# A transformer block on one core: values two groups behind the scores, the first half of the output projection between the last two, and the next layer norm moved ahead of the feed-forward

## The reference

```python
x = x + _L0_xattn_ref(_layernorm(x), ctx, ctx, Wq, Wk, Wv, Wo, lam, g)
x = x + _L0_ffn_ref(_layernorm(x), ln1_g, ln1_b, w1, b1, ln2_g, ln2_b, w2, b2)
```

## Time and profile before

| | us |
|---|---|
| median of 3 runs (2399.65 to 2402.44) | 2401.85 |
| the profiled execution's own time | 2400.83 |
| its span, first to last instruction | 2399.0 |
| busy: TensorE / VectorE / ScalarE / GpSimd | 2150.0 / 1804.7 / 1510.4 / 1047.7 |
| mean granted share of TensorE's clock | 0.953 |

### The profile page before, as it was taken

How to read it: one execution, slowest core, us unless ns; L and a number is a source line. 1 busy time by engine, 2 the same in 40 slices (tenths; PEclk the granted TensorE clock), 3 DMA queues, 4 the chain that set the end, 5 groups by cost and what they waited for, 6 DMA issues and landing times.

```text
span 2399.0 us, 45089 instructions
## 1 busy us (share of the span) xinstructions
PE 2150.0 (90%) x18239; PEld 1188.0 (50%) x18239; DVE 1804.7 (75%) x2722; ACT 1510.4 (63%) x1973; POOL 1047.7 (44%) x803
## 2 busy tenths in 40 slices
PE   7777899999899999999999999999989899999978
PEld 5444455554455555454545545455544545555443
DVE  4676778777787878778787878878687777867763
ACT  3575676656577665657766565766756576675644
POOL 2301715437182543718154371816346181634507
PEclk9868999999899999999999999999999999999989
DMA  8313113130411314031141303122141312312010
GB/s 292 109 47 81 44 55 80 24 108 22 112 47 54 80 24 108 23 98 46 54 95 25 108 22 97 46 71 72 37 104 20 97 46 70 72 37 72 2 53 18
DMA packets 253007, 160.14 MB, mean 67 GB/s; under 512 B 171812, under 2 KB 221580, under 8 KB 252288
## 3 DMA queue, kind: packets, MB, share of 16 engines
q1 hardware_dynamic: 249792, 152.07, 24.4%
q0 software_dynamic: 3008, 5.20, 0.7%
HBM read 51.82 MB, written 20.38 MB: 30 GB/s over the span
## 4 chain that ended last, share of the span: by engine, by line
PE 46%; POOL 23%; DVE 13%; ACT 8%; issue 5%; DMA 3%; SPq 1%; POOLq 0%; DVEq 0%; ACTq 0%
POOL attn_raw L684 21%; PE ps L1613 10%; PE ps L1444 5%; PE ps L1445 5%; PE ps L1597 5%; PE ps L1446 5%; DVE attn_raw L1143 3%; PE ps L1532 3%; DVE arena L1272 2%; DMA rows<-attn_raw 2%; ACT arena L808 2%; ACT attn_raw L811 2%; DVE attn_raw L1157 1%; ACT arena L806 1%; POOL attn_raw L680 1%
## 5 line engine op out<-in xcount | busy, mean ns | idle before, releaser
L684 POOL TENSOR_TENSOR attn_raw<-attn_raw 128x512 f32<-128x512 f32 x448 | 658.1, 1488 | 47.9 <-ACT attn_raw L836 18.1
L662 POOL TENSOR_TENSOR q<-q 128x512 f16<-128x512 f32 x128 | 169.3, 1327 | 763.6 <-ACT q L797 762.3
L1597 PE MATMUL ps<-rows,w1T 128*128 128x512 f16 x2048 | 486.4, 380 | 2.2 <-DVE rows L1232 2.2
L1113 DVE TENSOR_REDUCE arena<-ps 128x6 f32<-128x924 f32 (+1 forms) x308 | 328.5, 1081 | 30.4 <-PE ps L1500 28.5
L1613 PE MATMUL ps<-w2T,arena 128*128 128x512 f16 x1440 | 338.5, 390 | 0.0
L1597 PEld LDWEIGHTS ps<-rows,w1T 128*128 128x128 f16 x2048 | 195.4, 98 | 211.9 <-issue 3.3
L831 ACT ACTIVATE attn_raw<-ps,vec_cols,wstep 128x512 f32<-128x512 f32 x256 | 198.1, 774 | 148.7 <-PE ps L1597 145.2
L1237 DVE SCALAR_TENSOR_TENSOR arena<-attn_raw,vec_cols,arena 128x512 f16<-128x512 f32 x256 | 244.0, 953 | 43.1 <-ACT arena L834 41.8
L806 ACT ACTIVATE arena<-ps 128x1024 f32<-128x1024 f32 x128 | 130.8, 1022 | 218.5 <-PE ps L1532 218.5
L1143 DVE TENSOR_TENSOR attn_raw<-arena,attn_raw 128x1024 f16<-128x1024 f32 (+1 forms) x128 | 202.5, 1593 | 71.0 <-ACT attn_raw L811 64.1
L795 ACT ACTIVATE q<-ps 128x512 f32<-128x512 f32 x128 | 76.9, 601 | 270.0 <-PE ps L1446 269.9
(11 more groups left out here) (192 smaller groups left out, 4674.3 us busy)
## 6 DMA issues: line engine op xcount, KB each, us to landing
stack_raw<-q SPq DMA_DIRECT2D x744, 64.0 KB, 2.0
arena<-in_x SPq DMA_DIRECT2D x64, 256.0 KB, 3.1
out<-arena SPq DMA_DIRECT2D x64, 256.0 KB, 2.3
arena<-in_x SPq DMA_DIRECT2D x14, 1024.0 KB, 5.9
arena<-in_L_ffn_w SPq DMA_DIRECT2D x7, 1024.0 KB, 14.7
rows<-in_x SPq DMA_DIRECT2D x2, 1024.0 KB, 7.2
stack_raw<-in_L_xattn_Wq SPq DMA_DIRECT2D x8, 256.0 KB, 9.5
k_att<-k_store SPq DMA_DIRECT2D x4, 495.0 KB
```

Source lines behind the costliest of these rows:

```text
L684: ins = pool.tensor_tensor(acc[:, e, :], acc[:, e, :], src[:, j % NG, :], ALU.add)
L1113: dve.tensor_reduce(negmax[:, tt:tt + 2, u0:u1], ps[:, bank:bank + 2, 0:(u1 - u0) * S].rearrange("p b (u s) -> p b u s", s=S), AX.X, ALU.m ...
L1597: ins = pe.matmul(ps[:, B_H + j % 2, :], w1T[:, k, j * P:(j + 1) * P], rows16[:, e, k, :], start=(k == 0 and e == 0), stop=(k == KD - 1 an ...
```

## The change

1. `ATTEND`: values stand two groups behind the scores. VectorE's low halves of the probabilities have a token of their own (`l`). The exponentials of a group wait for the low halves two groups back (the float32 buffer) and the copies wait for the values two groups back (the float16 buffer); before, the exponentials waited for the values. Query 1 stands beside query 0, and the waits of queries 1 and 2 and of the late feed-forward product change with it.
2. TensorE does the output projection of pairs 0 and 1, for all four row tiles, between values 6 and values 7, once the last exponentials have read the scores' banks; then pair 2, then pair 3.
3. The additions of the last row tile of block i-1 (`y3`, `z3`) move into `mid_rows`, behind the mean square; its store and reload follow, and the reloads have a semaphore for each row tile.
4. The layer norm of block i+2 (all statistics, power, offsets, `ln1_rows`, `x_rows_hi`, `x_rows_lo`) moves out of the feed-forward: VectorE does statistics and offsets ahead of line 1201's sums and the low halves between the normalised rows and `h_lo`; ScalarE does rows and high halves ahead of query 4's copy; GpSimd takes that power ahead of the second layer norm's.
5. `MAXIMA_AT` and `TLAST`: four row scores beside each of the first three hidden tiles, none beside the last two; the maxima are split a tile earlier.
6. SyncE: pair 1's stacking follows the transposition of pair 1; x_in and the reload of tile 2 are issued before the transposition of pair 2; the keys of a new batch after that of pair 3.

```diff
@@ -62,7 +62,8 @@
 ATTEND = [(w[0], int(w[1:] or 0)) for w in (
-    "c e1 g y0 y1 s0 e2 q0 s1 v0 h1 s2 h2 y2 v1 s3 q1 t0 z0 z1 v2 s4 h3 v3 s5 h4 y3 t1 v4 s6 q2 z2 z3 v5 s7 q3 v6 t2 v7").split()]
+    "c e1 g y0 y1 s0 l0 e2 q0 s1 l1 q1 s2 v0 l2 h1 s3 v1 l3 h2 t0 y2 z0 z1 s4 v2 l4 q2 z2 s5 v3 l5 q3 t1 s6 v4 l6 h3 "
+    "s7 v5 l7 h4 v6 t2 v7").split()]
@@ -72,10 +73,6 @@
 NG = 3
-LN1_ROWS_AT = {2: (0,), 3: (1,), 4: (2,), 5: (3,)}
-X_HI_AT = {6: (0,), 7: (1,), 8: (2,), 9: (3,)}
-X_LO_AT = {7: (0,), 8: (1,), 9: (2,), 10: (3,)}
-
 def tokens(text):
@@ -86,7 +83,7 @@
 POOL_PROLOGUE = tokens("q0 q1 p0 q2 q3 p1 q4 q5 p2 q6 q7 p3")
-FIRST = tokens("r1 w0 s0 b0 w1 s1 x1 w2 v0 w3 s2 q0 w4 v1 w5 s3 w6 v2 w7 s4 q1 t0 w8 v3 w9 s5 q2 w10 v4 s6 t1 w11 v5 s7 q3 w12 v6 t2 "
+FIRST = tokens("r1 w0 s0 l0 b0 w1 s1 l1 x1 w2 v0 w3 s2 l2 q0 w4 v1 w5 s3 l3 w6 v2 w7 s4 l4 q1 t0 w8 v3 w9 s5 l5 q2 w10 v4 s6 l6 t1 w11 v5 s7 l7 q3 w12 v6 t2 "
                "w13 v7 w14 w15")
@@ -96,8 +93,8 @@
 VECTORS_AT = (1, 2, 3, 5, 6)
-MAXIMA_AT = (2, 2, 2, 4, 2, 4, 4, 2, 4, 2, 4, 4, 2, 4, 2, 0)
-TLAST = JH - 2
+MAXIMA_AT = (4, 4, 4, 2, 4, 2, 4, 2, 4, 2, 4, 2, 4, 2, 0, 0)
+TLAST = JH - 3
 PAIR = 2 * UPT
@@ -320,8 +317,9 @@
-        s_xin, s_xres, s_katt, s_vatt = (sem(n) for n in (
-            "x_in_loaded", "x_res_loaded", "k_att_loaded", "v_att_loaded"))
+        s_xres = [sem(f"x_res_loaded{tt}") for tt in range(TT)]
+        s_xin, s_katt, s_vatt = (sem(n) for n in (
+            "x_in_loaded", "k_att_loaded", "v_att_loaded"))
         s_st1, s_ag1, s_var1, s_rstd1, s_xhat1 = (sem(n) for n in (
@@ -508,7 +506,7 @@
                     wait(sp, s_stored[tt], c, 16, 0)
-                sp.dma_start(x_res[:, tt, :], x_blk[c][:, tt, :]).then_inc(s_xres, 16)
+                sp.dma_start(x_res[:, tt, :], x_blk[c][:, tt, :]).then_inc(s_xres[tt], 16)
@@ -551,15 +549,8 @@
             def iteration(i):
-                for what, n in ATTEND if i else ():
-                    if what == "z":
-                        store(i - 1, n)
-                        if n:
-                            load_x_res(i, n - 1)
-                    elif what == "t":
-                        transpose_attn(i, n)
-                        if n == 0 and i + 1 < NBLK:
-                            stack_queries(i + 1, 0, i)
+                ahead, ahead2 = i < NBLK - 1, i < NBLK - 2
+                keys_next = ahead and (i + 1) % BLK_PER_BATCH == 0
                 if i == 0:
@@ -567,24 +558,35 @@
                     transpose_ternary(JH + 12)
-                if i + 1 < NBLK and (i + 1) % BLK_PER_BATCH == 0:
-                    load_keys((i + 1) // BLK_PER_BATCH)
-                if i:
-                    load_x_res(i, TT - 1)
-                else:
-                    transpose_attn(i, KD - 2)
-                if i + 2 < NBLK:
-                    load_x_in(i + 2)
-                if i == 0:
+                    transpose_attn(0, 2)
+                    load_x_in(2)
                     for n in range(13, JH):
                         transpose_ternary(JH + n)
+                else:
+                    for what, n in ATTEND:
+                        if what == "z":
+                            store(i - 1, n)
+                            if n:
+                                load_x_res(i, n - 1)
+                        elif what == "t":
+                            if n == 2:
+                                load_x_res(i, TT - 2)
+                                if ahead2:
+                                    load_x_in(i + 2)
+                            transpose_attn(i, n)
+                            if n < 2 and ahead:
+                                stack_queries(i + 1, n, i)
                 transpose_attn(i, KD - 1)
-                if i + 1 < NBLK and (i + 1) % BLK_PER_BATCH == 0:
+                if i:
+                    store(i - 1, TT - 1)
+                    load_x_res(i, TT - 1)
+                if keys_next:
+                    load_keys((i + 1) // BLK_PER_BATCH)
                     load_values((i + 1) // BLK_PER_BATCH)
-                if i + 1 < NBLK:
-                    for p in range(1 if i else QATT // 2, QM // 2):
+                if ahead:
+                    for p in range(QATT // 2, QM // 2):
                         stack_queries(i + 1, p, i)
-                    if i + 2 < NBLK:
+                    if ahead2:
                         transpose_rows(i + 2)
@@ -695,13 +697,13 @@
                 power(1, s_var2, s_rstd2, i)
+                if ahead2:
+                    power(0, s_var1, s_rstd1, i + 2)
                 power_half(i, 0)
                 wait(pool, s_xhat2, i, TT, TT)
-                if ahead2:
-                    power(0, s_var1, s_rstd1, i + 2)
                 if ahead:
@@ -802,12 +804,14 @@
                 if gi >= 2:
-                    wait(act, s_pv, c, QM, gi - 1)
+                    wait(act, s_p_lo, c, QM, gi - 1)
                 act.activation(probs[:, buf, 0:2, :], ps[:, 0:2, :], ACT.Exp).then_inc(s_p, 1)
                     wait(act, s_p, c, 2 * QM, 2 * gi + half + 1)
+                    if gi >= 2:
+                        wait(act, s_pv, c, QM, gi - 1)
                     act.copy(split[:, 0, slices, :], probs[:, buf, slices, :]).then_inc(s_p_hi, 1)
@@ -889,6 +893,9 @@
                 load_table(ACT.Gelu)
+                if ahead2:
+                    ln1_rows(i + 2, range(TT))
+                    x_rows_hi(i + 2, range(TT))
                 if ahead:
@@ -898,10 +905,6 @@
                     gelu(i, j)
-                    if ahead2 and j in LN1_ROWS_AT:
-                        ln1_rows(i + 2, LN1_ROWS_AT[j])
-                    if ahead2 and j in X_HI_AT:
-                        x_rows_hi(i + 2, X_HI_AT[j])
                 load_table(ACT.Exp)
@@ -1188,16 +1191,19 @@
                 rms_variance(c)
+                if c:
+                    add_ffn(c - 1, TT - 1, ffn_bank(TT - 1))
+                    add_shift(c - 1, TT - 1)
                 if ahead2:
-                    ln1_stats(c + 2, (0, 1))
+                    ln1_stats(c + 2)
                 wait(dve, s_rstd2, c, 1, 1)
                 wait(dve, s_rsc, c, 1, 1)
-                wait(dve, s_xres, c, 16 * TT, 16 * TT)
                 def mid(half):
                         wait(dve, s_wo, c, TT, tt + 1)
+                        wait(dve, s_xres[tt], c, 16, 16)
                         dve.scalar_tensor_tensor(x_res[:, tt, :], ps[:, tt, :], rms_scale[:, tt:tt + 1],
@@ -1217,6 +1223,8 @@
+                if ahead2:
+                    ln1_offsets(c + 2)
                 mid(0)
@@ -1278,7 +1286,7 @@
                 for what, n in ATTEND if i else FIRST:
-                    if what == "s":
+                    if what == "l":
                         probs_lo(i, n)
@@ -1301,10 +1309,8 @@
                 if ahead2:
-                    ln1_stats(i + 2, (2, 3))
+                    x_rows_lo(i + 2, range(TT))
                 h_lo(i)
-                if ahead2:
-                    ln1_offsets(i + 2)
                 for j in range(JH):
@@ -1312,8 +1318,6 @@
                     row_maxima(i + 1, beside[2:])
-                    if ahead2 and j in X_LO_AT:
-                        x_rows_lo(i + 2, X_LO_AT[j])
                     if ahead and j == TLAST:
@@ -1460,17 +1464,14 @@
                         wait(pe, s_q32, c, QM, n - 1)
-                elif n == 0 and c >= 2:
+                elif n < 2 and c >= 2:
                     wait(pe, s_p, c - 1, 2 * QM, 2)
                 elif n == 1:
-                    if c >= 2:
-                        wait(pe, s_y, c - 2, TT, 3)
-                    else:
-                        wait(pe, s_q32, c, QM, n)
+                    wait(pe, s_q32, c, QM, n)
                 elif 2 <= n < 4:
                     if n == 2 and c >= 2:
-                        wait(pe, s_y, c - 2, TT, TT)
+                        wait(pe, s_y, c - 2, TT, 3)
                 elif n == 4:
@@ -1603,10 +1604,12 @@
                         wait(pe, s_p, c + 1, 2 * QM, 2)
+                        if c + 2 < NBLK:
+                            wait(pe, s_q32, c + 2, QM, 2)
                     elif j == 0 and tt == 3:
                         if c + 2 < NBLK:
-                            wait(pe, s_q32, c + 2, QM, 2)
+                            wait(pe, s_q32, c + 2, QM, 4)
                     elif tt == 1:
@@ -1646,6 +1649,10 @@
                     elif what == "v":
+                        if n == QM - 1:
+                            wait(pe, s_p, i, 2 * QM, 2 * QM)
+                            for tt in range(TT):
+                                out_projection(i, tt, (0, 1))
                         values(i, n)
@@ -1656,10 +1663,9 @@
                         queries(i + 1, n)
-                for tt in range(TT):
-                    out_projection(i, tt, (0, 1, 2))
-                for tt in range(TT):
-                    out_projection(i, tt, (3,))
+                for pairs in ((2,), (3,)):
```

(2 more changed lines are left out.)

## The result

| | before | after |
|---|---|---|
| median (us) | 2401.74, 4 runs, 2399.65 to 2402.44 | 2359.34, 4 runs, 2356.36 to 2361.55 |
| profiled execution / its span (us) | 2400.83 / 2399.0 | 2361.55 / 2359.7 |
| mean granted share of TensorE's clock | 0.953 | 0.957 |

The ratio is 0.9824, with a 95% interval of 0.9809 to 0.9838: the change makes the kernel 1.8% faster. I had forecast 2396.6, in a range of 2362 to 2417. The forecast was wrong and the range missed by 3 us. Rival (a), "line 1097 meets no query", gave 2367.

The account below looks back on a forecast made before the run. TensorE was taken to bound the cycle up to the last values, GpSimd the feed-forward. Middle blocks +0.45 us each, times 13 = +5.9, with the end blocks in all -5.2: median 2401.85 to 2396.6 us, range 2362 to 2417.

Parts of the forecast that it names:

- Rival (a): Ahead of the hidden tiles: VectorE's rows' low halves meet no GpSimd query, -1.8 us a block, 2367 us; chance 0.25.
- Values find their group normalised: Attention: with scores two groups ahead, the waits of 0.85 and 4.28 us in front of values go.
- V7 at 60.1: Last group of values: starts 60.1 us into the cycle instead of 59.72, taking 2.05 us at full clock instead of 2.9.
- A wait of 3.9 us ahead of pair 3: Behind the last values: TensorE has 2.6 us of matmuls until pair 3's transposition lands at 6.5 us, and idles 3.9.
- done by about 51 us against 55 when that is ready: nothing: SyncE's queue: pair 1's 12 copies, 7.7 us of issue, move ahead of pair 2's transposition without delaying it.
- VectorE becomes the bound behind V7, line 1201 at E+10.4, no wait for TensorE: Residual sum: the moved layer norm holds VectorE until 10.4 us after the last values end; pair 3 allowed it from 8.
- so I take 2.5 + 2 x 1.1 = 4.7, to E+24.5: Rows' four low halves on VectorE: two meetings with GpSimd's queries make 4.7 us, ending 24.5 us after the last values.
- The clock at the hidden tiles: First hidden tiles: TensorE standing still about 3 us before them may lower its clock; bounds 0 and 1.7 us, taken 0.3.
- rival (b): Ahead of the first hidden tile: TensorE's new idle time drops the clock, +1.7 us a block, 2413 us; chance 0.25.
- Feed-forward at 51.5: Feed-forward stretch: GpSimd's work falls from 46.24 to 44.37 us, two delays of 0.4; net -1.1, to 51.5 us.
- splitting the maxima one tile earlier ... I cost it at nothing: End of feed-forward: the earlier split lets the last low half through before GpSimd ends; cost nothing, under GpSimd's cover.
- The ends: Blocks outside the middle thirteen: block 0 -4.5 us (-1 to -8), block 14 -1.6, block 15 -5.

Follow-up runs that it names:

- run 1: The kernel after, with the output projection of pairs 0 and 1 put back behind the last values, pairs 0 to 2 in one piece: 2393.07 us, ratio 0.9959 to before.
- run 6: The kernel after, with the output projection wholly behind the last values in three steps (pairs 0 and 1, pair 2, pair 3): 2343.21 us, ratio 0.9754 to before.
- run 4: The kernel after, with the old spread of row scores and the old place of the maxima's split: 2340.87 us, ratio 0.9763 to before.
- run 8: The kernel after, with the projection behind the last values in three steps and the load of x behind pair 2's transposition: 2306.39 us, ratio 0.9599 to before.
- run 5: The kernel after, with GpSimd no longer waiting for the normalised rows before the low halves of queries 5 to 7: 2386.16 us, ratio 0.9935 to before.

## Why the prediction was wrong

The mechanism was followed rightly up to one term, and that term carried the sign.

- **Values find their group normalised.** Right: no wait of values for a normalised group in the middle cycles.
- **V7 at 60.1.** Measured 59.55 on average, 0.55 sooner. Its 2.05 us at full clock are right (2.06).
- **A wait of 3.9 us ahead of pair 3.** Right in size: 3.3 to 3.5 us in eleven cycles of thirteen (1.6 and 2.0 in the others), though in many a part of it, up to 1.4, stands ahead of pair 2, which I had costed at nothing. The sentence "done by about 51 us against 55 when that is ready: nothing" looked at SyncE's issue and not at what the transfers do to the landing, 6.1 us instead of 2.7. It cost nothing here because the projection and V7 covered it, as runs 1 and 6 show. It decided every experiment that took that cover away.
- **VectorE becomes the bound behind V7, line 1201 at E+10.4, no wait for TensorE.** Right: E+10.1, no wait. The normalised rows end at E+19.5 against E+19.8.
- **The failed step: "so I take 2.5 + 2 x 1.1 = 4.7, to E+24.5".** The term was mis-sized: it measured 2.49 us, to E+21.9, and the hidden tiles started at E+23.3 instead of E+25.85. I charged each meeting 1.1 us of VectorE's time, after two crossed rows of before in which each engine waited for one instruction of the other (1.75 and 1.73). They did meet, but VectorE was first and held GpSimd out through all four, so that the two meetings cost VectorE nothing. The same four took no longer than free in runs 1, 4, 6, 8 and 9. Run 5 shows what a meeting costs at another place: there the engines took turns, VectorE paid 1.7 us a cycle, and the time went to 2386.16. Why the engines take turns in one place and not in the other is not shown. Of the cycle's miss of 3.2 us (139.8 expected, 136.56 measured) this step is 2.3, the rows' end before it 0.3, V7's place 0.55 and the clock 0.3; the feed-forward gives 0.15 back.
- **The clock at the hidden tiles.** I took 0.3 us, and rival (b) 1.5. TensorE idled 0.48 us ahead of them, not 3, so the question never came up; the granted clock behind is 1.00, as the window of after shows:

```profile
1884.53:1894.00 9.47, 8.95 (x65) 5.12 (x66) 8.15 (x10) 6.72 (x11) 4.64 (x4) 1.00 0.33 85
```

- **Feed-forward at 51.5.** Right on average, 51.66. GpSimd's stretch, with the rows' work gone, is 44.59 against 46.24:

```profile
1891.15:1935.74 44.59, 39.48 (x28) 1.00 0.23 50
```

 But "splitting the maxima one tile earlier ... I cost it at nothing" went along with a spread that costs 18 us (run 4): I took its 0.4 us at the start of GpSimd's work, and neither the clock ahead of V7 nor the last blocks.
- **The ends.** Expected -11.2, measured -3.2. Block 0 won 3.6 as thought. Block 14, for which I had -1.6, lost 2.2, and block 15 won 1.8 instead of 5. Both come back with the old spread of the row scores (4.8 and 2.4 us shorter in run 4); I did not follow why.

Rival (a) came within 8 us (2367), for a reason that is half true: line 1097 lost nothing, but it did meet a query. That it came so near is in part luck, since the ends were 8 us worse than I had them and other terms of the cycle made up for it. "both are released by the same end of line 1226" was the argument against (a), and the trace confirms it; it only didn't have the consequence that I drew.

What the change's parts are worth, by the runs: the projection between V6 and V7 does not pay. The gain lies in the trailing values together with SyncE's order and the last row tile's additions (run 10, which has only these and the projection in three steps, is 85 us under before); the three were not tried apart. The projection fills a gap that the trailing values had already cut from 4.28 to 1.2 us with 5.2 us of matmuls, and takes them from the stretch behind V7, where TensorE has slack beside VectorE's 10 us. It does cover a late transposition, which comes from a load of x placed just ahead of it. With projection and load moved back together (run 8) the kernel is 53 us faster than after, and with the old spread of row scores as well (run 9) 61.5. The load moved back in after, and nothing else, was not tried.

## What to carry to other kernels

Before work is moved into a gap, take the gap that is left after the rest of the change, and ask which engine is the bound just behind: 5.2 us into a gap of 1.2 delayed V7 by 4.5 us a block here and made the stretch behind it only 0.7 shorter. When two engines meet at SBUF, ask who issues first, and do not price the meeting by one seen elsewhere: here it cost the engine on the path nothing at one place and 1.7 us at another. If only one of them is on the path, a wait on the other can settle the order. A transposition by DMA that someone waits for should have no large load issued just ahead of it on its queue, and an experiment that takes its cover away must look at its landing first.

## What the runs showed of the hardware

- Four of VectorE's two-input SBUF instructions back to back kept GpSimd out for the whole row of them: GpSimd's instruction of 1.15 us, issued 0.16 us behind the first, took 3.34 (VectorE's four 2.49 us in sum, each 0.68 to 0.69), in every block of after that prepares rows and in five further kernels.
- In other places the engines took turns. In before, GpSimd's low half got in between two such instructions of VectorE (1.73 us instead of 1.15, VectorE's second 2.71 instead of 1.76). In run 5, VectorE's pair of single-input instructions (line 1233) took 2.66 instead of 1.00 beside two of GpSimd's, each waiting for one. What makes the difference is not shown.
- A DMA transposition of an SBUF tile lands 2.7 us after its issue in the quiet case, and 4.9 to 8.2 us (after, runs 1 and 6) when a load of 1 MB and copies of queries were issued just ahead of it on the same queue; with the copies alone ahead (run 8), 2.8 to 5.2. By the time between the load of x and the transposition: 0.8 to 1.3 us behind the load, pair 3's took 6.0 to 6.8 us in before; 3.0 to 3.7 us behind, 2.7 to 4.5; 8.7 to 10.6 us behind, 2.7 to 2.8 in after.
- The granted clock at the start of attention falls in some cycles, to a mean of 0.81 over 5.3 us in the one shown, which costs 1.8 us of the cycle. A wait of TensorE of 0.69 us in front of small float32 matmuls goes with it in after, in six cycles of six with a wait of 0.69 us or more, but in before five of the eleven cycles with that wait kept 1.00. The wait alone does not decide it.
